# Scores of a wide cross attention on four 32 row strips of the tensor engine, exponentials by pairs of key tiles

## The chip, the cores and the metric

The program runs on one core of a Trainium2 chip, as one launch. Its time is the device time of that core in microseconds; the median of three runs is compared. The engines are named as in the profile: PE is the tensor engine's matmul stream and PEld its weight loads, DVE the vector engine, ACT the scalar engine, POOL GpSimd, SP the engine that issues most transfers. PSUM is the memory that PE writes: eight banks, each of 512 float32 columns.

## What is computed

The reference is a perceiver block: a masked cross attention of 64 latents on 1601 context rows, a gated attention, a quantized feed-forward stage, a second ("wide") cross attention, a laplacian attention, and routed experts. Only the second cross attention is touched:

```python
def _L1_xattn_ref(x, context, context_mask, Wq, Wk, Wv, Wo):
    q = (x @ Wq).reshape(B, N, HEADS, hd).transpose(0, 2, 1, 3)        # 32 batches, N = 64, 16 heads of 16
    k = (context @ Wk).reshape(B, M, HEADS, hd).transpose(0, 2, 1, 3)  # M = 1601, context of width 192
    v = (context @ Wv).reshape(B, M, HEADS, hd).transpose(0, 2, 1, 3)
    scores = jnp.einsum('bhid,bhjd->bhij', q, k) * scale
    scores = jnp.where(context_mask[:, None, None, :], scores, max_neg)
    attn = jax.nn.softmax(scores, axis=-1)
    out = jnp.einsum('bhij,bhjd->bhid', attn, v)
```

## The kernel before

The stages of the block are functions that follow one another with a barrier between them. `wide_cross_attention` is the fourth. It works through 32 batches; the 1601 keys of a batch are 13 tiles of 124 keys (the last has 113), and four chunks of 4, 3, 3 and 3 tiles for the work that goes by chunks. The 256 columns of keys and queries are two halves `o` of 128 rows, 8 heads in each.

For each batch these steps are done, named as in the table `ROUNDS` that sets the order on every engine:

- K(c): PE projects the keys of chunk c into two PSUM banks (five matmuls each), ACT copies them to `khi`, rounded to float32r (a float32 format that PE reads in one pass), DVE writes the rest that was rounded off to `klo`. V0, V1: the values, evicted by ACT into `val`.
- S, X: ACT and DVE split the context of a later batch into the same two parts. Q, Q1, Q2: mask count, `qhi`, `qlo`.
- A(c), c = 0 to 15: scores by `qhi` and `khi` alone, queries as rows, for the maxima. One A is two matmuls (k = 0, 1) of 64 rows each, the upper and the lower half of the array, into two banks; DVE reduces each bank to a column of maxima ("max" below, line 2016).
- mred, M: DVE makes the negated maxima in two bfloat16 parts, PE transposes them (four 128x128 transposes), ACT copies them to `augq`.
- B(t), t = 0 to 12: the exact scores of one key tile, keys as rows, 1024 columns (16 heads of 64 queries) in two banks. Two bfloat16 matmuls of 512 columns lay down mask and maximum (`augk`, `augq`); twelve float32r matmuls of 256 columns add `khi*qhi`, `khi*qlo` and `klo*qhi`. They alternate between the two 64 row halves of the array. ACT takes the exponential into one of four buffers `P`.
- PV(t): 16 heads by `val`, summed in the bank `acc`. F0, F1, F2: the division.

The banks are split so: `sc` is two buffers of two banks, so that B(t+1) is written while ACT reads B(t); `ring` is three banks that K, V, A, M and F1 fill in turn, each fill after the reader of the third fill before it is done (`FILLS`, `room`); `acc` is one. The order is the same on all engines, with B of batch n next to A, K, V of batch n+1 and S, X, Q of batch n+2. The steps that the prediction speaks of stand in these rows of `ROUNDS`:

```python
("Ln", 0), ("Ln", 1), ("A", 0), ("B", 0), ("A", 1), ("B", 1), ("A", 2), ("X", 2), ("K", 1), ("F1", 0), ("PV", 0),
("A", 3), ("B", 2), ("A", 4), ("B", 3), ("S", 3), ("K", 2), ("V0", 0), ("F2", 0), ("Q2", 0), ("PV", 1), ("PV", 2),
("A", 5), ("B", 4), ("A", 6), ("B", 5), ("A", 7), ("X", 3), ("V1", 0), ("V0", 1), ("PV", 3), ("PV", 4),
("A", 8), ("B", 6), ("A", 9), ("B", 7), ("A", 10), ("Sn", 0), ("K", 3), ("V1", 1), ("Qn", 0), ("PV", 5), ("PV", 6),
("A", 11), ("B", 8), ("A", 12), ("B", 9), ("Xn", 0), ("Sn", 1), ("V0", 2), ("V1", 2), ("PV", 7), ("PV", 8),
("A", 13), ("B", 10), ("A", 14), ("B", 11), ("A", 15), ("Sn", 2), ("V0", 3), ("V1", 3), ("mred", 0), ("PV", 9), ("PV", 10),
("B", 12), ("Q1n", 0), ("Xn", 1), ("Kn", 0), ("M", 0), ("PV", 11), ("PV", 12), ("F0", 0)
```

They are called row 1 to row 7 of the schedule below. Each engine takes its own steps from them in this order and waits on semaphores for the others.

## Time and profile before

| | |
|---|---|
| median of three runs | 3859.05 us (3858.34 to 3862.12) |
| the profiled execution | 3861.68 us, of which 3859.9 us between its first and last instruction |
| wide cross attention in it | from about 1900 to 3326 us |
| PE busy over the span | 3103.3 us, 80% |
| DVE, ACT, POOL | 2558.5 us (66%), 1975.3 us (51%), 641.2 us (17%) |

Busy time of PE counts overlapping matmuls once, and the end of a matmul in the trace is modelled. The kernel is a sequence of stages with different limits, so the shares over the whole span say little of one stage; the sections of the trace below are from the wide cross attention, and one from the first cross attention.

### The profile page before, as it was taken

Reading aid. Unit: us, or ns where it says so; the run is one execution under the profiler, and the core shown is the slowest. Engines: PE = TensorE matmul, PEld = TensorE weight load, DVE = VectorE, ACT = ScalarE, POOL = GpSimd, SP = SyncE. Lnnn points to the kernel's source line nnn. Section 1 sums busy time; section 2 is a strip of 40 time slices with the busy share of each in tenths; the row PEclk is TensorE's granted clock in tenths of the full one; section 3 lists DMA queues with packets and bytes.
Section 4 is the critical chain, followed back from the end, with each engine's and each line's share of the span. In section 5 each row is a group of like instructions: output and inputs, shape, how many; then the busy total and the mean of one; then the engine's idle time right before and its main releaser. Section 6 shows DMA issues by size and latency. Waiting matters only on the chain. (4 is left out here: it accounts for less than half of the span.)

```text
span 3859.9 us, 99037 instructions
## 1 busy us (share of the span) xinstructions
PE 3103.3 (80%) x34558; PEld 2704.9 (70%) x34558; DVE 2558.5 (66%) x7485; ACT 1975.3 (51%) x4178; POOL 641.2 (17%) x768
## 2 busy tenths in 40 slices
PE   3449999999999976666399999999999999653574
PEld 3348888888888864444178888888888888542453
DVE  5558888888888845667477777776777777455000
ACT  1146666666766642333146666666666666321111
POOL 0223233233333310000211111111111111000101
PEclk7669999999999986776589999999999999865787
DMA  2132233232233210000111111111111111212511
GB/s 64 51 85 82 81 82 83 80 84 80 79 85 80 78 51 27 14 22 17 38 38 39 41 40 40 40 39 40 38 39 41 39 38 29 73 44 83 180 48 61
DMA packets 235435, 221.25 MB, mean 57 GB/s; under 512 B 69516, under 2 KB 228545, under 8 KB 234816
## 3 DMA queue, kind: packets, MB, share of 16 engines
q1 hardware_dynamic: 232896, 208.22, 19.1%
q0 software_dynamic: 2048, 6.68, 0.5%
q8 instruction: 284, 4.65, 0.5%
q14 instruction: 207, 1.70, 0.1%
HBM read 186.30 MB, written 28.39 MB: 56 GB/s over the span
## 5 line engine op out<-in xcount | busy, mean ns | idle before, releaser
L2016 DVE CUSTOM_DVE_ANT_0 xb_junk<-xb_ring,xb_mbias 128x372 bf16<-128x372 f32 (+2 forms) x1024 | 544.2, 573 | 176.2 <-PE xb_ring L1924 155.3
L1855 ACT ACTIVATE xb_P<-xb_sc 124x1024 f32<-124x1024 f32 (+1 forms) x416 | 426.2, 1027 | 374.5 <-PE xb_sc L1948 372.3
L879 PE MATMUL xa_acc<-xa_raw,xa_P 124*128 124x193 f32 x1664 | 315.6, 330 | 7.2 <-ACT xa_P L754 7.2
L1895 PE MATMUL xb_ring<-xb_xst,xb_whi 128*128 128x372 f32 (+2 forms) x768 | 262.2, 369 | 38.1 <-DVE xb_xst L1995 32.5
L1924 PE MATMUL xb_ring<-xb_khi,xb_qhi 64*128 64x372 f32 (+2 forms) x1024 | 269.0, 404 | 26.6 <-DVE xb_klo L2001 17.3
L1895 PE MATMUL xb_ring<-xb_whi,xb_xst 128*124 128x256 f32 (+1 forms) x1248 | 285.1, 291 | 2.8 <-DVE xb_maxes L2016 0.4
L1948 PE MATMUL xb_sc<-xb_qhi,xb_khi 64*124 64x256 f32 (+1 forms) x1664 | 281.9, 372 | 0.0
L879 PEld LDWEIGHTS xa_acc<-xa_raw,xa_P 124*128 124x128 f32 x1664 | 266.4, 189 | 18.6 <-ACT xa_P L754 12.1
L2001 DVE TENSOR_TENSOR xb_klo<-xb_ring,xb_khi 128x372 fp32r<-128x372 f32 (+2 forms) x256 | 138.6, 571 | 208.8 <-ACT xb_khi L1821 207.8
L865 PE MATMUL xa_sc<-xa_qblk,xa_kT 128*124 128x128 f32 x1664 | 238.6, 272 | 0.0
L1895 PEld LDWEIGHTS xb_ring<-xb_whi,xb_xst 128*124 128x124 f32 (+1 forms) x1248 | 215.8, 187 | 23.1 <-DVE xb_maxes L2016 15.8
L1963 PE MATMUL xb_acc<-xb_P,xb_val 124*17 124x64 f32 x13312 | 229.8, 220 | 0.5 <-ACT xb_P L1855 0.5
L1963 PEld LDWEIGHTS xb_acc<-xb_P,xb_val 124*17 124x17 f32 x13312 | 190.6, 97 | 39.2 <-issue 15.9
L1895 PE MATMUL xb_ring<-xb_wlo,xb_xst 128*124 128x256 f32 (+1 forms) x832 | 217.5, 283 | 0.0
L865 PEld LDWEIGHTS xa_sc<-xa_qblk,xa_kT 128*124 128x124 f32 x1664 | 215.7, 186 | 0.1
L672 POOL CAST xa_kTr<-xa_kT 128x744 fp32r<-128x744 f32 (+1 forms) x128 | 110.1, 860 | 620.1 <-ACT xa_kT L740 620.1
L1948 PE MATMUL xb_sc<-xb_qlo,xb_khi 64*124 64x256 f32 (+1 forms) x1664 | 203.3, 278 | 0.0
L1948 PE MATMUL xb_sc<-xb_qhi,xb_klo 64*124 64x256 f32 (+1 forms) x1664 | 203.1, 277 | 0.0
L1948 PEld LDWEIGHTS xb_sc<-xb_qhi,xb_khi 64*124 64x124 f32 (+1 forms) x1664 | 193.7, 182 | 11.6 <-issue 0.2
L1944 PE MATMUL xb_sc<-xb_augq,xb_augk 64*124 64x512 bf16 (+1 forms) x832 | 199.6, 385 | 0.0
L1924 PEld LDWEIGHTS xb_ring<-xb_khi,xb_qhi 64*128 64x128 f32 x1024 | 151.3, 186 | 65.9 <-DVE xb_klo L2001 29.5
L1895 PEld LDWEIGHTS xb_ring<-xb_xst,xb_whi 128*128 128x128 f32 x768 | 145.6, 192 | 72.2 <-issue 39.3
(435 smaller groups left out, 8342.4 us busy)
## 6 DMA issues: line engine op xcount, KB each, us to landing
xa_raw<-in_ctx SPq DMA_DIRECT2D x64, 279.0 KB
ex_w<-in_W SPq DMA_DIRECT2D x16, 1024.0 KB, 10.0
xa_raw<-in_ctx SPq DMA_DIRECT2D x32, 372.0 KB
xa_xTr<-in_ctxT SPq DMA_DIRECT2D x64, 186.0 KB
xb_raw<-in_ctxT SPq DMA_DIRECT2D x64, 186.0 KB, 2.4
xa_xTr<-in_ctxT SPq DMA_DIRECT2D x32, 248.0 KB, 2.7
xb_raw<-in_ctxT SPq DMA_DIRECT2D x32, 248.0 KB
xa_mask<-in_mask SPq DMA_DIRECT2D x32, 200.1 KB, 5.4
```

Source lines behind the costliest of these rows:

```text
L672: nc.gpsimd.tensor_copy(kTr[:, c % 2, :, 0:W], kT[:, p, :, k0:k0 + W]).then_inc(sem("kTr"), 1)
L865: i = nc.tensor.matmul(s_[0:w, 256 * u + 128 * o:256 * u + 128 * o + 128], kt[:, o, :], qblk[:, t3, o, :], start=False, stop=True, skip_gr ...
L879: i = nc.tensor.matmul(acc[:, o, :], w, raw[0:KEYS, t3, t, :], start=t == 0 and o == 0, stop=t == NKT - 1, skip_group_check=True)
L1855: nc.scalar.activation(P[0:w, pbuf(c, p), :], sc[(c + p) % 2][0:w, :], ACT.Exp).then_inc(sem("exped"), 1)
L1895: i = nc.tensor.matmul(out, l, r, start=k == 0, stop=k == 4)
L1924: i = nc.tensor.matmul(bank[:, 0:w], qhi[half, p, o, 128 * s:128 * s + 128], khi[half, p, o, k0:k0 + w], start=True, stop=True)
L1944: nc.tensor.matmul(s[0:w, 512 * k:512 * k + 512], augk[half, p, keys], augq[half, p, :], start=True, stop=True)
L1948: i = nc.tensor.matmul(s[0:w, 512 * k + 256 * o:512 * k + 256 * o + 256], kk[half, p, o, keys], q[half, p, o, :], start=False, stop=True, ...
L1963: i = nc.tensor.matmul(acc[32 * j:32 * j + VW, 64 * g:64 * g + 64], val[0:w, p, c, h, :], P[0:w, pbuf(c, p), place(h):place(h) + 64], star ...
L2001: v.tensor_tensor(klo[:, p, o, k0:k0 + w], ring[f % 3][:, 0:w], khi[:, p, o, k0:k0 + w].bitcast(F32), ALU.subtract).then_inc(sem("klo"), 1)
L2016: v.tensor_tensor_reduce(out=junk[:, k, 0:w], in0=ring[f % 3][:, 0:w], in1=mbias[:, p, k0:k0 + w], scale=1.0, scalar=-3.0e38, op0=ALU.add, ...
```

## The change

The query rows of B are narrowed from 64 to 32: in each 32 row strip of the array only two heads have their rows, so a matmul needs 128 query columns instead of 256, and four strips (`strip`, `rows`) hold what two halves held. One tile of B is then four bfloat16 matmuls of 256 columns and 24 float32r matmuls of 128 columns, in rounds of four, one in each strip. The four strips write four banks. All four banks of the old two buffers are one buffer `sc` of four banks, and a key tile has half of each bank: the even tile of a pair the columns 0 to 255, the odd tile the columns 256 to 511. PE signals ACT once for a pair of tiles (`NPAIR` = 7 signals a batch), after its second tile; ACT then takes the two exponentials; PE starts the next pair when both are done. A uses the 32 row strips too (still two matmuls of the same columns). M is two transposes instead of four, `augq` has 256 columns instead of 512. The mask row of `augk` is written in four strips by POOL, one after the other, instead of two, and so are its rows of ones at the stage's start.

```diff
-        sc = [m.psum(f"sc{k}", [128, 1024]) for k in range(2)]
+        sc = m.psum("sc", [128, 4, 512])
...
             if not (isinstance(value, int) and value <= 0):
                 engine.wait_ge(sem(name), value)
 
+        def strip(k, s):
+
+            return 2 * k + s
+
+        def rows(r):
+
+            return slice(32 * r, 32 * r + 32)
+
         def place(h):
 
             g, j = h // 4, h % 4
-            return 512 * (g % 2) + 256 * (g // 2) + 64 * j
+            return 256 * strip(g % 2, j // 2) + 128 * (g // 2) + 64 * (j % 2)
 
         block = ctx.enter_context(nc.Block())
 
...
             pool.wait_ge(sem("set"), 1)
-            nc.gpsimd.memset(augk[0:2, :, :], 1.0).then_inc(sem("set"), 1)
-            pool.wait_ge(sem("set"), 2)
-            nc.gpsimd.memset(augk[64:66, :, :], 1.0).then_inc(sem("set"), 1)
-            pool.wait_ge(sem("set"), 3)
-            for k in range(2):
-                nc.gpsimd.memset(negmax[:, :, 64 * k + 32:64 * k + 33], 1.0)
+            for r in range(4):
+                nc.gpsimd.memset(augk[32 * r:32 * r + 3, :, :], 1.0).then_inc(sem("set"), 1)
+                pool.wait_ge(sem("set"), 2 + r)
+            for r in range(4):
+                nc.gpsimd.memset(negmax[:, :, 32 * r:32 * r + 1], 1.0)
             nc.gpsimd.memset(val[:], 1.0).then_inc(sem("set"), 1)
-            pool.wait_ge(sem("set"), 4)
+            pool.wait_ge(sem("set"), 6)
 
             def step(kind, c, n, p):
                 if kind == "Q":
...
-                        pool.wait_ge(sem("s_ps"), (n - 1) * NKT)
+                        pool.wait_ge(sem("s_ps"), (n - 1) * NPAIR)
                     wait_apart(pool)
-                    for k, r in enumerate((32, 96)):
+                    for k in range(4):
+                        r = 32 * k
                         nc.gpsimd.tensor_scalar(augk[r:r + 1, p, :], mask8[r:r + 1, :], -1.0, some[r:r + 1, 1:2], ALU.add, ALU.mult).then_inc(sem("augk"), 1)
-                        pool.wait_ge(sem("augk"), nth(n, 2, k))
+                        pool.wait_ge(sem("augk"), nth(n, 4, k))
                         wait_apart(pool)
             schedule(step, pool)
 
...
-                if kind == "B":
-                    w = KEYS if c < NKT - 1 else LAST
-                    act.wait_ge(sem("s_ps"), nth(n, NKT, c))
-                    upto(act, "pv", nth(n, NKT, c - back(c, p)))
-                    nc.scalar.activation(P[0:w, pbuf(c, p), :], sc[(c + p) % 2][0:w, :], ACT.Exp).then_inc(sem("exped"), 1)
+                if kind == "B" and (c % 2 or c == NKT - 1):
+                    act.wait_ge(sem("s_ps"), nth(n, NPAIR, c // 2))
+                    for t in range(c - c % 2, c + 1):
+                        w = KEYS if t < NKT - 1 else LAST
+                        upto(act, "pv", nth(n, NKT, t - back(t, p)))
+                        half = slice(256 * (t % 2), 256 * (t % 2) + 256)
+                        nc.scalar.activation(P[0:w, pbuf(t, p), :].rearrange("p (r n) -> p r n", r=4), sc[0:w, :, half], ACT.Exp).then_inc(sem("exped"), 1)
                 if kind == "F0":
 
                     act.wait_ge(sem("pv"), nth(n, NKT, NKT - 1))
...
                     pe.wait_ge(sem("qhi"), nth(n, 1, 0))
                     for k in range(2):
-                        half = slice(64 * k, 64 * k + 64)
+                        r = rows(strip(k, s))
                         bank = room((kind, c, k), n)
-                        i = nc.tensor.matmul(bank[:, 0:w], qhi[half, p, o, 128 * s:128 * s + 128], khi[half, p, o, k0:k0 + w], start=True, stop=True)
+                        i = nc.tensor.matmul(bank[:, 0:w], qhi[r, p, o, 128 * s:128 * s + 128], khi[r, p, o, k0:k0 + w], start=True, stop=True)
                         i.then_inc(sem("a_ps"), 1)
                 if kind == "M":
                     pe.wait_ge(sem("negmax"), nth(n, 1, 0))
                     bank = room((kind, c, 0), n)
-                    for a in range(4):
+                    for a in range(2):
                         i = nc.tensor.transpose(bank[:, 128 * a:128 * a + 128], negmax[:, a, :], ident[:])
                     i.then_inc(sem("m_ps"), 1)
                 if kind == "B":
-                    s = sc[(c + p) % 2]
                     w = KEYS if c < NKT - 1 else LAST
                     keys = slice(c * KEYS, c * KEYS + w)
+                    at = 256 * (c % 2)
                     if c == 0:
                         pe.wait_ge(sem("augq"), nth(n, 1, 0))
-                        pe.wait_ge(sem("augk"), nth(n, 2, 1))
+                        pe.wait_ge(sem("augk"), nth(n, 4, 3))
                         pe.wait_ge(sem("qlo"), nth(n, 1, 0))
                         pe.wait_ge(sem("klo"), nth(n, 8, 7))
-                    upto(pe, "exped", nth(n, NKT, c - 2))
-                    halves = [slice(64 * k, 64 * k + 64) for k in range(2)]
-                    for k, half in enumerate(halves):
-                        nc.tensor.matmul(s[0:w, 512 * k:512 * k + 512], augk[half, p, keys], augq[half, p, :], start=True, stop=True)
+                    if c % 2 == 0:
+                        upto(pe, "exped", nth(n, NKT, c - 1))
+                    for r in range(4):
+                        nc.tensor.matmul(sc[0:w, r, at:at + 256], augk[rows(r), p, keys], augq[rows(r), p, :], start=True, stop=True)
                     for kk, q in ((khi, qhi), (khi, qlo), (klo, qhi)):
                         for o in range(2):
-                            for k, half in enumerate(halves):
-                                i = nc.tensor.matmul(s[0:w, 512 * k + 256 * o:512 * k + 256 * o + 256], kk[half, p, o, keys], q[half, p, o, :],
+                            for r in range(4):
+                                i = nc.tensor.matmul(sc[0:w, r, at + 128 * o:at + 128 * o + 128], kk[rows(r), p, o, keys],
+                                                     q[rows(r), p, o, 128 * (r % 2):128 * (r % 2) + 128],
                                                      start=False, stop=True, skip_group_check=True)
-                    i.then_inc(sem("s_ps"), 1)
+                    if c % 2 or c == NKT - 1:
+                        i.then_inc(sem("s_ps"), 1)
                 if kind == "PV":
 
                     w = KEYS if c < NKT - 1 else LAST
```

On PE, two A steps and the B between them at the start of row 4 (A8, B6, A9; the names are output<-inputs, the last pair rows x columns that are written, x the count of equal ones). Before:

```order
L1963 MATMUL xb_acc<-xb_P,xb_val 17x64 x32
L1924 MATMUL xb_ring<-xb_khi,xb_qhi 128x372 x2
L1944 MATMUL xb_sc<-xb_augq,xb_augk 124x512 x2
L1948 MATMUL xb_sc<-xb_qhi,xb_khi 124x256 x4
L1948 MATMUL xb_sc<-xb_qlo,xb_khi 124x256 x4
L1948 MATMUL xb_sc<-xb_qhi,xb_klo 124x256 x4
L1924 MATMUL xb_ring<-xb_khi,xb_qhi 128x372 x2
```

and of the change:

```order
L1977 MATMUL xb_acc<-xb_P,xb_val 17x64 x32
L1936 MATMUL xb_ring<-xb_khi,xb_qhi 128x372 x2
L1956 MATMUL xb_sc<-xb_augq,xb_augk 124x256 x4
L1960 MATMUL xb_sc<-xb_qhi,xb_khi 124x128 x8
L1960 MATMUL xb_sc<-xb_qlo,xb_khi 124x128 x8
L1960 MATMUL xb_sc<-xb_qhi,xb_klo 124x128 x8
L1936 MATMUL xb_ring<-xb_khi,xb_qhi 128x372 x2
```

Nothing stands in another place; B's instructions are twice as many and half as wide. On ACT, rows 4 and 5 of the schedule from the exponentials of B6 and B7 to the value evictions V0(2) and V1(2). The waits are named by the first use of a reused semaphore: here `lp_a_rstd1` is `s_ps`, PE's signal that scores are done, and `lp_qk_ps1` is `pv`, that a buffer `P` is free. Before:

```order
L1855 ACTIVATE xb_P<-xb_sc 124x1024 [waits lp_qk_ps1,lp_a_rstd1] x2
L1812 ACTIVATE xb_xst<-xb_raw 128x496 [waits lp_lT0,lp_x_in1]
L1813 ACTIVATE xb_xst<-xb_raw 64x496
L1821 ACTIVATE xb_khi<-xb_ring 128x362 [waits lp_b_rstd1] x2
L1849 ACTIVATE xb_val<-xb_ring 124x16x16 [waits lp_lT0]
```

and of the change:

```order
L1867 ACTIVATE xb_P<-xb_sc 124x1024 [waits lp_qk_ps1,lp_a_rstd1]
L1867 ACTIVATE xb_P<-xb_sc 124x1024 [waits lp_qk_ps1]
L1822 ACTIVATE xb_xst<-xb_raw 128x496 [waits lp_lT0,lp_x_in1]
L1823 ACTIVATE xb_xst<-xb_raw 64x496
L1831 ACTIVATE xb_khi<-xb_ring 128x362 [waits lp_b_rstd1] x2
L1859 ACTIVATE xb_val<-xb_ring 124x16x16 [waits lp_lT0]
```

Each of the two exponentials waited for its own tile; now the first waits for the whole pair, and the second for no scores at all. What stands behind them on ACT is the same.

## Rows read from the trace of the kernel before

**Rows 1.** The page, busy time by engine.

```profile
PE 3103.3 (80%) x34558; PEld 2704.9 (70%) x34558; DVE 2558.5 (66%) x7485; ACT 1975.3 (51%) x4178; POOL 641.2 (17%) x768
```

**Rows 2.** Windows: stretch, length, busy us (count) by engine, granted clock, DMA share, GB/s.

```profile
2750.00:3050.00 300.00, 295.30 (x5261) 261.60 (x5261) 214.01 (x633) 194.72 (x311) 37.56 (x36) 1.00 0.15 39
```

**Rows 3.** Timeline of PE, M of two batches (start, us from first to last), and M's line.

```profile
2573.33 0.60 PE L1930 MATMUL xb_ring<-xb_ident,xb_negmax 128*128 128x128 f32 x4
...
2616.20 0.60 PE L1930 MATMUL xb_ring<-xb_ident,xb_negmax 128*128 128x128 f32 x4
...
L1930 PE MATMUL xb_ring<-xb_ident,xb_negmax x128: 270/272/328, 1977.5 to 3301.2; 128*128 128x128 f32 x128
```

**Rows 4.** Groups by line and shape, 2000 to 3300 us (busy us, mean ns | idle before).

```profile
L1948 PE MATMUL xb_sc<-xb_qlo,xb_khi 64*124 64x256 f32 x1460 | 182.1, 278 | 0.0
...
L1963 PEld LDWEIGHTS xb_acc<-xb_P,xb_val 124*17 124x17 f32 x11712 | 167.9, 97 | 36.5 <-issue 15.0
...
L1948 PEld LDWEIGHTS xb_sc<-xb_qlo,xb_khi 64*124 64x124 f32 x1460 | 147.4, 182 | 0.0
```

**Rows 5.** Timeline of PE in the last batch, where B follows B.

```profile
3308.79 0.43 PE L1944 MATMUL xb_sc<-xb_augq,xb_augk 64*124 64x512 bf16 x2
...
3309.29 0.40 PE L1948 MATMUL xb_sc<-xb_qlo,xb_khi 64*124 64x256 f32 x4
...
3309.77 0.38 PE L1944 MATMUL xb_sc<-xb_augq,xb_augk 64*124 64x512 bf16 x2
...
3311.81 0.43 PE L1944 MATMUL xb_sc<-xb_augq,xb_augk 64*124 64x512 bf16 x2
```

**Rows 6.** First cross attention, two float32r matmuls of 64 columns, 128 columns of weights each.

```profile
L844 PE MATMUL xa_ring<-xa_klTr,xa_qblkr x64: 191/264/402, 266.3 to 1399.6; 128*128 128x64 f32 x64
...
924.62 0.30 PE L844 MATMUL xa_ring<-xa_klTr,xa_qblkr 128*128 128x64 f32 x2
```

**Rows 7.** Timeline of ACT in rows 4 and 5 of the schedule.

```profile
2597.91 1.03 ACT L1855 ACTIVATE xb_P<-xb_sc 124x1024 f32<-124x1024 f32 x1 [0.18 <-PE xb_sc L1948]
2598.84 0.61 ACT L1812 ACTIVATE xb_xst<-xb_raw 128x496 fp32r<-128x496 f32 x1
...
2599.85 0.81 ACT L1821 ACTIVATE xb_khi<-xb_ring 128x362 fp32r<-128x362 f32 x2
...
2604.15 1.03 ACT L1855 ACTIVATE xb_P<-xb_sc 124x1024 f32<-124x1024 f32 x1 [0.17 <-PE xb_sc L1948]
...
2605.88 0.85 ACT L1849 ACTIVATE xb_val<-xb_ring 124x512 f32<-124x512 f32 x2
```

**Rows 8.** Timeline of DVE there, and from the first max of row 1 of the schedule.

```profile
2595.92 0.55 DVE L2016 CUSTOM_DVE_ANT_0 xb_junk<-xb_ring,xb_mbias 128x372 bf16<-128x372 f32 x1 [1.65 <-PE xb_ring L1924]
...
2597.48 0.54 DVE L2016 CUSTOM_DVE_ANT_0 xb_junk<-xb_ring,xb_mbias 128x372 bf16<-128x372 f32 x1
...
2600.34 0.98 DVE L2001 TENSOR_TENSOR xb_klo<-xb_ring,xb_khi 128x362 fp32r<-128x362 f32 x2 [1.21 <-ACT xb_khi L1821]
...
2618.47 0.67 DVE L2016 CUSTOM_DVE_ANT_0 xb_junk<-xb_ring,xb_mbias 128x496 bf16<-128x496 f32 x1 [0.78 <-PE xb_ring L1924]
...
2623.93 1.00 DVE L2001 TENSOR_TENSOR xb_klo<-xb_ring,xb_khi 128x372 fp32r<-128x372 f32 x2
```

**Rows 9.** Timeline of PE in row 4 of the schedule: A8, A9, K3, A11.

```profile
2595.31 0.43 PE L1924 MATMUL xb_ring<-xb_khi,xb_qhi 64*128 64x372 f32 x2
...
2596.50 0.46 PE L1924 MATMUL xb_ring<-xb_khi,xb_qhi 64*128 64x372 f32 x2
...
2598.08 0.44 PE L1895 MATMUL xb_ring<-xb_xst,xb_whi 128*128 128x362 f32 x1
...
2601.55 0.44 PE L1924 MATMUL xb_ring<-xb_khi,xb_qhi 64*128 64x372 f32 x2
```

**Rows 10.** Timelines of POOL and PE at the start of the stage.

```profile
1910.43 2.76 POOL L1768 MEMSET xb_augk<- 2x3204 bf16 x1
...
1928.13 0.75 PE L1895 MATMUL xb_ring<-xb_xst,xb_whi 128*128 128x496 f32 x1 [32.55 <-DVE xb_xst L1995]
```

More of the change, by code:

```diff
@@ L1803, in _ @@
             nc.scalar.activation(whi[:], w_raw[:], ACT.Copy).then_inc(sem("whi"), 1)
-            act.wait_ge(sem("set"), 4)
+            act.wait_ge(sem("set"), 6)
             def step(kind, c, n, p):
@@ L1836, in step @@
                     if not (isinstance(n, int) and n < 2):
-                        act.wait_ge(sem("s_ps"), (n - 1) * NKT)
-                    nc.scalar.activation(augq[:, p, :], ring[f % 3][:], ACT.Copy).then_inc(sem("augq"), 1)
+                        act.wait_ge(sem("s_ps"), (n - 1) * NPAIR)
+                    nc.scalar.activation(augq[:, p, :], ring[f % 3][:, 0:256], ACT.Copy).then_inc(sem("augq"), 1)
                 if kind in ("V0", "V1"):
@@ L1984, in _ @@
             v.tensor_tensor(wlo[:], w_raw[:], whi[:].bitcast(F32), ALU.subtract).then_inc(sem("wlo"), 1)
-            dve.wait_ge(sem("set"), 4)
+            dve.wait_ge(sem("set"), 6)
             def step(kind, c, n, p):
@@ L2017, in step @@
                                                scale=1.0, scalar=-3.0e38, op0=ALU.add, op1=ALU.max,
[L2018 removed]
+                                               accum_out=maxes[:, p, 4 * o + strip(k, s), c // 4:c // 4 + 1]).then_inc(sem("maxed"), 1)
                 if kind == "mred":
```

20 lines of the change are left out of this document (11 added, 9 removed).

## Prediction

> **What bounds the kernel now.** I read the engines' shares first [rows 1], then the same by stretch: in the wide cross attention PE is busy 295 of 300 us at full clock (1.00 granted), DVE 214, ACT 195 [rows 2]. So there PE sets the time, and a batch is its work: M of one batch starts 42.87 us after M of the one before [rows 3]. The reader is to see one more thing, in the timelines: PE's margin over DVE is thin. In row 4 of the schedule K3 starts at 2598.08, 0.06 us after the max of A9's second bank ended (2597.48 + 0.54), the bank three fills before it in the ring [rows 8, 9]. From A8 to K3 PE already runs in step with DVE.
>
> **B, the tile of scores.** Where B follows B a tile takes 3309.77 - 3308.79 = 0.98 us [rows 5]. Four float32r matmuls, two rounds of two halves, take 0.40 with 0.28 for one [rows 4, 5], so a round is 0.12: 256 columns at 2.4 GHz are 0.107. Six rounds are 0.71; 0.27 is left for the bfloat16 pair of 512 columns and the turn to the next tile. Afterwards a round is four matmuls of 128 columns. If the stream set its length it would be 0.06 and B would fall by 6 x 0.06 and half of 0.213 for the bfloat16 round, 0.46 us in all. But every matmul loads 124 columns of weights first. A load of 17 such columns takes 97 ns, one of 124 takes 182 [rows 4]: 0.79 ns a column, 0.1 us for 124 however many rows it has. One place shows whether it hides: two float32r matmuls of only 64 columns, with 128 columns of weights, take 0.30 together and 0.19 is the shortest single one [rows 6], so the second ends 0.11 after the first, where its stream is 0.03. The load is not hidden. I take 0.105 to 0.11 for a round in all four strips at once: B becomes 0.98 - 0.107 - 6 x 0.01 = 0.81, 0.17 less. The bounds: 0.46 less (stream), 0.11 less (rounds stay at 0.12, only the bfloat16 part gains), and, as no row shows four strips loading at once, rounds of two loads in turn, 0.22, which is 0.5 more.
>
> The Trainium skill says the same of the load: by "TensorE: Matmul & The Clock Gate", section "LDWEIGHTS (loading the stationary operand)", it takes the columns of weights divided by 1.2 per ns, and 32 rows cost what 128 cost. By it the round is 0.103, and B's gain 0.2; the trace agrees, and the rule speaks against a change that halves streams and doubles loads.
>
> **M.** Two transposes of (0.60 - 0.27)/3 = 0.11 fewer [rows 3], 0.22 a batch. If all this reached the end: 13 x 0.17 + 0.22 = 2.4 us a batch, 77 us in 32. It does not, for three reasons.
>
> **DVE is next.** One max is issued every 0.47 us (2595.92 to 2597.48 is three of them with 0.15 idle) [rows 8], an A every 0.94, and A8 to A9 is 1.19, later ones 1.10 [rows 9]. With B shorter PE comes at 0.94 to 1.03 and meets DVE. In rows 3, 4 and 6 of the schedule (three A, two B) the step behind the last A waits for a max whose time is that of the first plus three intervals: only the 0.15 idle goes, not 0.33. Row 1 (496 columns, 0.60 each) is DVE's wholly: its maxes, X2 and klo run without a gap from 2618.47 to 2624.93 [rows 8], so B0 and B1 gain nothing there. What moves it is when A0's first max starts, and M's 0.22 and B12's 0.17 do come before that, as far as klo of Kn0 lets A0 go.
>
> **The pair on ACT.** Before, ACT took the first exponential while PE made the second tile. Row 4: exponential of B7 at 2597.91, two S copies from 2598.84, khi of K3 at 2599.85 to 2600.66, klo of K3 at 2600.34 to 2601.32, and A11 at 2601.55, which may fill the bank that klo frees [rows 7 to 9]: 0.23 us of slack for its second matmul. After, both exponentials start behind B7: 0.93 from one to the next (2597.91 to 2598.84), and B7's end comes 0.2 to 0.3 sooner. ACT's chain is later by 0.93 - 0.3 = 0.6 to 0.7, so A11's second half starts 0.4 to 0.5 later than now. B8 and B9 (0.33 shorter) give most of that back. Then the same in row 5: exponentials of B8 and B9, S, eviction of V0(2) (now 2605.88 to 2606.5) come 0.5 to 0.6 later, while A13, which needs that bank, could go 0.2 sooner: A13's second half is 0.1 to 0.3 late. In rows 2 and 7 the delay is covered by V0 and by PV.
>
> Going through the seven rows, against now: row 1 -0.2 (M's part), row 2 -0.4 at K2, of which Q2 and klo, held up by ACT, leave 0.1 at A5's max; row 3 0; row 4 and 5 together +0.1 to +0.35 at A13; row 6 -0.35 (PE and DVE catch up); row 7 -0.2 (B12) and -0.2 (M, part of it behind klo). A batch becomes 0.3 to 0.8 us shorter, I take 0.53: 30 batches of the steady part, **-16 us**.
>
> **What is added outside.** POOL sets the rows of ones in four pieces of 2.76 us instead of two [rows 10]; DVE and ACT wait for POOL's last signal and PE for them; its first matmul of the stage comes at 1928.13 after 32.55 us of idling: +5.5 us, all exposed, and two more mask rows by POOL beside DVE's first X steps, +0.3. **+6**. In the last batch there is no A to fill PE: a pair of B with its two PV is 3311.81 - 3308.79 = 3.02 us now [rows 5]. Then it is two B, 1.6, the signal 0.2, two exponentials 0.93 + 1.03 [rows 7], and the way back 0.1: 3.7 to 3.8. Six pairs by 0.7: **+4**. The two mask rows that POOL adds in each batch (1.6 us each) start after B12 and end before X2, in PSUM-fed work of DVE: nothing; if DVE's X2 stood in the same time it would pay some tenths of a us a batch.
>
> Sum: -16 + 6 + 4 = -6. The profiled execution took 3861.7 (span 3859.9 and 1.8 around it), so 3855.7 there; the median is 2.6 under that execution: **3853 us**. A difference under 0.2%, 7.7 us, is what a measurement of this kernel can't tell from none, and the forecast is within it.
>
> **Rivals.**
> - Loads hide, so a round costs its stream, 0.06. For it: the halves of B now overlap loads with streams wholly (0.12 a round with loads of 0.1 in it). Against it: rows 6. Then B is 0.52; PE reaches B7, B9 and B3 0.3 to 0.6 sooner, the ACT chains start sooner too, and only DVE's pace and row 1 hold: about 1.9 us a batch, -57, with 10 outside: 3812. Chance 0.07. The Trainium skill has a measured gain for this packing ("TensorE: Matmul & The Clock Gate", "Measured speedup vs the span model": four strips of 32 rows, 512 columns, 3.07 times); by it a round of four here would take 4/3.07 of one stream, 0.07 us, and the sum would be near this rival's, but its streams are four times as long as these.
> - Rounds stay at 0.12, so that B gives 0.11 only, and the pair's delay on ACT shows. Its place is A11 and A13. 0.06 less in each of the seven B's that count and some tenths more wait: 0.4 to 0.6 us a batch, 15 us back: 3868. Slower as soon as a round is 0.12 or an exponential over four half banks takes 0.1 longer than 1.03. Chance 0.18.
> - Four strips do not load together, rounds of 0.2: B 0.3 to 0.5 longer, 4 to 6 us a batch, of which ACT and DVE waits absorb a part: 3980. Chance 0.07.
> - POOL's mask rows or the waits on ACT's queue cost what I set at nothing, beyond row 4 and 5: 0.5 to 1.5 us a batch, 3870 to 3900. Chance 0.1.
>
> **How the numbers follow.** The forecast has 0.58. Its own range is 0.3 to 0.8 us a batch with 10 us outside: 3843 to 3862. In it I give faster (under 3851) 0.45, the same 0.47, slower 0.08. With the rivals: faster 0.26 + 0.07 + 0.02, the same 0.27 + 0.03, slower the rest: 0.35, 0.3, 0.35. Range: it leaves out the serial loads and the hidden loads: 3825 to 3895.
>
> **What would show it.** B beside B at 0.8 (0.5 or 1.0 and more would be a rival); pairs of exponentials 0.93 apart, each pair behind its second tile; PE waiting at A11 and A13 for klo and for V's eviction, at A5, V1 and K3 for maxes; PE's share of the stage falling to some 93%; PE's first matmul of the stage 6 us later; the last batch's pairs 3.75 apart. The prediction is wrong if PE's period falls by over a microsecond, which rows 6 do not allow, or if a wait of ACT's chain repeats in more rows than two.

## The result and the profile after

The changed kernel takes 3870.22 us, median of 13 runs (3863.89 to 3872.02), for 3860.25 us (3856.77 to 3865.34, 13 runs) of the kernel before on the same chip: ratio 1.0023, 95% interval 1.0015 to 1.0032. I had forecast 3853 and no measurable difference. It is slower by 0.15 to 0.32 per cent. The profiled execution took 3867.97 us (span 3866.2), 6.3 more than that of before.

What I read first is whether the mechanism that I had costed is there. The timeline of PE in the last batch, where B follows B, and one row of ACT:

```profile
3306.80 0.33 PE L1956 MATMUL xb_sc<-xb_augq,xb_augk 32*124 32x256 bf16 x4
...
3307.34 0.39 PE L1960 MATMUL xb_sc<-xb_qhi,xb_klo 32*124 32x128 f32 x8
3307.56 0.28 PE L1956 MATMUL xb_sc<-xb_augq,xb_augk 32*124 32x256 bf16 x4
...
3310.48 0.33 PE L1956 MATMUL xb_sc<-xb_augq,xb_augk 32*124 32x256 bf16 x4 [0.27 <-ACT xb_P L1867]
...
3308.49 1.94 ACT L1867 ACTIVATE xb_P<-xb_sc 124x1024 f32<-124x1024 f32 x2 [1.17 <-PE xb_sc L1960]
```

B to B is 3307.56 - 3306.80 = 0.76 us (0.98 in [rows 5]; forecast 0.81). A pair is 3310.48 - 3306.80 = 3.68 (3.02 before; forecast 3.7 to 3.8). The two exponentials of the row, 1.02 us each, start 0.92 apart. All this is near the forecast. Then the steady part, by M's starts, the windows around one of them (columns as in [rows 2]), and the windows of the whole stretch:

```profile
2840.31 0.38 PE L1942 MATMUL xb_ring<-xb_ident,xb_negmax 128*128 128x128 f32 x2
...
2882.29 0.38 PE L1942 MATMUL xb_ring<-xb_ident,xb_negmax 128*128 128x128 f32 x2
...
2925.38 0.38 PE L1942 MATMUL xb_ring<-xb_ident,xb_negmax 128*128 128x128 f32 x2
```

```profile
2880.00:2893.10 13.10, 12.52 (x244) 10.34 (x245) 9.75 (x26) 7.02 (x13) 6.41 (x4) 1.00 0.18 46
...
2893.20:2896.60 3.40, 3.40 (x15) 3.40 (x14) 0.51 (x2) 3.26 (x6) 0.00 (x0) 0.50 0.02 5
...
2896.70:2920.00 23.30, 22.85 (x565) 19.98 (x564) 17.84 (x55) 13.65 (x22) 2.04 (x3) 1.00 0.21 44
...
2750.00:3050.00 300.00, 290.74 (x6526) 252.53 (x6526) 215.72 (x641) 186.99 (x314) 59.14 (x49) 0.99 0.16 40
```

The first batch takes 41.98 us, the second 43.09, and in the second the granted clock is 0.50, that is 1.2 GHz, from 2893.2 to 2896.6, where PE is busy without a break. PE's busy time went from 295.30 to 290.74 of 300 [rows 2], 97% where the forecast had named some 93% as a sign, and the clock's mean went below 1.00, where it had stayed before. The trace's record of the clock has eight such stretches between the first and the last M, outside the turn of the loop; that of before has none.

The turn of the loop (14 batches a pass, two passes) is the other place. PE's first matmul behind it, of before and then of after, and the clock behind it:

```profile
2664.47 0.64 PE L1924 MATMUL xb_ring<-xb_khi,xb_qhi 64*128 64x496 f32 x2 [4.08 <-issue]
```

```profile
2669.36 0.88 PE L1936 MATMUL xb_ring<-xb_khi,xb_qhi 32*128 32x496 f32 x2 [7.25 <-issue]
```

```profile
2664.60:2678.00 13.40, 8.64 (x81) 7.45 (x85) 6.33 (x17) 2.90 (x4) 0.91 (x1) 0.50 0.03 6
2688.50:2691.80 3.30, 3.30 (x18) 3.30 (x17) 2.25 (x7) 2.09 (x3) 0.00 (x0) 0.50 0.41 79
```

PE idles 7.25 us for 4.08, and the half clock in this batch lasts 17.1 us for 3.4. Last, POOL's ones and PE's first matmul of the stage:

```profile
1909.79 11.22 POOL L1777 MEMSET xb_augk<- 3x3204 bf16 x4
...
1935.99 0.75 PE L1907 MATMUL xb_ring<-xb_xst,xb_whi 128*128 128x496 f32 x1 [38.02 <-DVE xb_xst L2009]
```

The four strips of ones take 11.22 us together, and PE idles 38.02 us for 32.55 [rows 10]: 5.5 more, as forecast. The first M comes 81.8 us after the stage's start for 77.7.

From these views a ledger of the stage, changed less before, in the two profiled executions:

- The median of batches in which the clock stayed full is 42.07 us for 42.51: 29 batches by -0.44 = -12.8.
- The batch with the turn takes 53.37 for 48.34: +5.0.
- What the other batches have above their median (after: six with a slow stretch, each 1.0 to 1.5; before: small excesses) is 7.5 for 2.1: +5.4.
- Sum between first and last M: -2.4 (1321.1 for 1323.4). First M +4.1, from the last M to the end +3.6. The stage takes 1431.9 for 1426.5 us.

### The profile page after: what moved, and what is told of

Same layout as the page of the kernel before. It is cut to its first block and busy times, and to the rows that moved or that the text cites. A ratio compares the mean times of both kernels' runs of the same rounds, so it can differ in the third digit from the quotient of the medians.

```text
span 3866.2 us, 110572 instructions
## 1 busy us (share of the span) xinstructions
PE 3073.6 (79%) x40318; PEld 2657.7 (69%) x40318; DVE 2562.6 (66%) x7485; ACT 1933.5 (50%) x4178; POOL 749.8 (19%) x836
## 5 line engine op out<-in xcount | busy, mean ns | idle before, releaser
L1867 ACT ACTIVATE xb_P<-xb_sc 124x1024 f32<-124x1024 f32 (+1 forms) x416 | 405.8, 1024 | 470.6 <-PE xb_sc L1960 470.6
L2031 DVE CUSTOM_DVE_ANT_0 xb_junk<-xb_ring,xb_mbias 128x372 bf16<-128x372 f32 (+2 forms) x1024 | 533.9, 572 | 121.3 <-PE xb_ring L1936 116.0
L1936 PE MATMUL xb_ring<-xb_khi,xb_qhi 32*128 32x372 f32 (+2 forms) x1024 | 350.1, 427 | 48.0 <-DVE xb_klo L2015 22.4
L1804 POOL TENSOR_SCALAR xb_augk<-xb_mask,xb_some 1x1602 bf16<-1x1602 uint8 x128 | 206.7, 1615 | 264.1 <-PE xb_sc L1960 247.5
L1936 PEld LDWEIGHTS xb_ring<-xb_khi,xb_qhi 32*128 32x128 f32 x1024 | 170.0, 184 | 123.7 <-DVE xb_klo L2015 46.3
L1960 PE MATMUL xb_sc<-xb_qhi,xb_khi 32*124 32x128 f32 (+1 forms) x3328 | 241.0, 283 | 0.0
L1960 PE MATMUL xb_sc<-xb_qlo,xb_khi 32*124 32x128 f32 (+1 forms) x3328 | 227.2, 266 | 0.0
L1960 PE MATMUL xb_sc<-xb_qhi,xb_klo 32*124 32x128 f32 (+1 forms) x3328 | 227.2, 266 | 0.0
L1907 PEld LDWEIGHTS xb_ring<-xb_xst,xb_whi 128*128 128x128 f32 x768 | 150.7, 199 | 73.2 <-issue 42.9
L1956 PE MATMUL xb_sc<-xb_augq,xb_augk 32*124 32x256 bf16 (+1 forms) x1664 | 199.6, 297 | 1.6 <-ACT xb_P L1867 1.6
```

The source lines that it names most:

```text
L1804: nc.gpsimd.tensor_scalar(augk[r:r + 1, p, :], mask8[r:r + 1, :], -1.0, some[r:r + 1, 1:2], ALU.add, ALU.mult).then_inc(sem("augk"), 1)
L1867: nc.scalar.activation(P[0:w, pbuf(t, p), :].rearrange("p (r n) -> p r n", r=4), sc[0:w, :, half], ACT.Exp).then_inc(sem("exped"), 1)
L1907: i = nc.tensor.matmul(out, l, r, start=k == 0, stop=k == 4)
L1936: i = nc.tensor.matmul(bank[:, 0:w], qhi[r, p, o, 128 * s:128 * s + 128], khi[r, p, o, k0:k0 + w], start=True, stop=True)
L1956: nc.tensor.matmul(sc[0:w, r, at:at + 256], augk[rows(r), p, keys], augq[rows(r), p, :], start=True, stop=True)
L1960: i = nc.tensor.matmul(sc[0:w, r, at + 128 * o:at + 128 * o + 128], kk[rows(r), p, o, keys], q[rows(r), p, o, 128 * (r % 2):128 * (r % 2) ...
```

## The experiments

All figures of all runs are in one table, since the runs answer each other. "Batch" is the median from M to M of batches at full clock, "slow" the number of stretches at half clock between first and last M outside turns of the loop, "steady" the time from the first M to the last, "stage" the whole fourth stage, all three in the profiled execution. The ratio is to the kernel before on the same chip. The runs come in sets, and the changed kernel was timed in one of them only; where it is compared with a kernel of another set, the difference of the ratios can stand up to 3 us from that of the medians, which the text gives. And a median holds more than the stage: the rest of the kernel, the same code in all sixteen, takes 2428 to 2438 us in the profiled executions (span less stage). Where the expectations count seven slow stretches for the changed kernel they leave out the first batch, and fourteen (e1_ones) and six (e7_both) count one more than the table.

| kernel | median us | ratio (95%) | batch | slow | first M | steady | stage |
|---|---|---|---|---|---|---|---|
| before | 3860.3 | | 42.51 | 0 | 77.7 | 1323.4 | 1426.5 |
| changed | 3870.2 | 1.0023 (1.0015 to 1.0032) | 42.07 | 8 | 81.8 | 1321.1 | 1431.9 |
| changed, ones at once (e1_ones) | 3859.8 | 0.9989 (0.9980 to 0.9998) | 42.01 | 13 | 71.3 | 1324.6 | 1425.0 |
| before, pairs alone (e2_pair_before) | 3907.4 | 1.0119 (1.0103 to 1.0134) | 43.89 | 0 | 76.9 | 1362.1 | 1470.6 |
| changed, no turn (e4_noturn) | 3846.9 | 0.9963 (0.9949 to 0.9977) | 41.87 | 7 | 81.8 | 1304.1 | 1414.9 |
| before, no turn (e5_noturn_before) | 3853.3 | 0.9977 (0.9968 to 0.9986) | 42.54 | 0 | 77.7 | 1317.6 | 1420.7 |
| changed, 64 columns (e3_cols64) | 3879.4 | 1.0042 (1.0027 to 1.0056) | 41.97 | 27 | 81.7 | 1339.0 | 1449.5 |
| changed, 62 keys (e6_keys62) | 3834.3 | 0.9923 (0.9908 to 0.9937) | 41.19 | 3 | 81.8 | 1286.3 | 1394.8 |
| changed, filled (e8_fill) | 3866.0 | 1.0014 (1.0005 to 1.0023) | 42.34 | 0 | 81.7 | 1317.7 | 1429.5 |
| changed, ones, no turn (e7_both) | 3845.8 | 0.9956 (0.9944 to 0.9969) | 41.85 | 5 | 71.3 | 1301.6 | 1402.0 |
| changed, 3 of 4 strips' exp. (e9_exp3) | 3827.6 | 0.9914 (0.9899 to 0.9929) | 40.94 | 4 | 81.3 | 1283.8 | 1391.7 |
| changed, X by two (e10_x2) | 3848.8 | 0.9969 (0.9957 to 0.9981) | 41.52 | 2 | 80.7 | 1297.8 | 1407.5 |
| before, ones, no turn (e11_both_before) | 3848.4 | 0.9968 (0.9956 to 0.9980) | 42.55 | 0 | 71.5 | 1317.6 | 1414.5 |
| changed, ones, no turn, a third filled (e12_best) | 3838.3 | 0.9942 (0.9928 to 0.9955) | 42.06 | 0 | 71.5 | 1302.0 | 1403.2 |
| changed, 4 batches a pass (e13_turn4) | 3905.9 | 1.0112 (1.0095 to 1.0129) | 42.06 | 8 | 81.8 | 1362.9 | 1473.7 |
| before, 4 batches a pass (e14_turn4_before) | 3884.3 | 1.0058 (1.0041 to 1.0074) | 42.52 | 0 | 77.7 | 1348.9 | 1452.0 |

**Changed, ones at once.**

```diff
-            nc.gpsimd.memset(augk[:], 0.0)
+            nc.gpsimd.memset(augk[:], 1.0)
...
-            for r in range(4):
-                nc.gpsimd.memset(augk[32 * r:32 * r + 3, :, :], 1.0).then_inc(sem("set"), 1)
-                pool.wait_ge(sem("set"), 2 + r)
```

> The changed kernel, with the rows of augk for the mask set by one memset of the whole tile to one instead of a memset to zero and four strips of ones (the rows between stand against rows of augq that are zero, so the scores are the same). If the four strips of ones (2.76 us each) stand on the path of the prologue, the first transposes M of the stage come 11 us after the stage's start sooner than in the changed kernel (81.7 us from start to M there, about 71 here) and the whole is 11 us faster, 3859. If the prologue is bound by loads or by X and K anyway, M comes at most 3 us sooner. The steady part must stay as it is (a batch 42.07 us).

The first M comes at 71.3 us, 10.5 sooner, and the median is 10.4 below the changed kernel's. The strips of ones are exposed almost wholly (11.22 us of them). The steady part didn't stay as it was: its batches have 13 slow stretches for 8 and it is 3.5 us longer, with the same instructions in it. So the number of slow stretches moves without any change to what PE does; that has to be kept in mind for every count below.

**Before, pairs alone.**

```diff
-                    act.wait_ge(sem("s_ps"), nth(n, NKT, c))
-                    upto(act, "pv", nth(n, NKT, c - back(c, p)))
-                    nc.scalar.activation(P[0:w, pbuf(c, p), :], sc[(c + p) % 2][0:w, :], ACT.Exp).then_inc(sem("exped"), 1)
+                    if c % 2 or c == NKT - 1:
+                        act.wait_ge(sem("s_ps"), nth(n, NKT, c))
+                        for t in range(c - c % 2, c + 1):
+                            w = KEYS if t < NKT - 1 else LAST
+                            upto(act, "pv", nth(n, NKT, t - back(t, p)))
+                            nc.scalar.activation(P[0:w, pbuf(t, p), :], sc[(t + p) % 2][0:w, :], ACT.Exp).then_inc(sem("exped"), 1)
...
-                    upto(pe, "exped", nth(n, NKT, c - 2))
+                    if c % 2 == 0:
+                        upto(pe, "exped", nth(n, NKT, c - 1))
```

> The kernel before, with one part of the change alone: exponentials by pairs (ACT takes two behind the second tile of a pair, PE waits for both before the next pair); the tiles of scores themselves stay on two halves of 64 rows, 0.98 us. If pairing is cheap in the steady part, because A and X stand between the B's, a batch stays within 0.2 us of 42.49 and only the last batch's pairs grow, from 3.02 to some 4.0 us, +6 us in all, about 3867. If the pair's delay on ACT is what ate the gain of the strips, a batch grows by 0.5 to 1 us, 15 to 30 us more: 3880 and over.

The second holds, and more than it says: pairs alone cost 1.38 us a batch, 45 us in all. The waits from 2000 to 3300 us (total us, times, longest), of before, with pairs alone, and of the changed kernel:

```profile
ACT xb_P L1855 <- PE xb_sc L1948: 357.7, 366, 5.9
...
DVE xb_klo L2001 <- ACT xb_khi L1821: 194.6, 122, 3.0
...
PEld xb_ring L1924 <- DVE xb_klo L2001: 26.3, 58, 0.9
```

```profile
ACT xb_P L1858 <- PE xb_sc L1952: 490.0, 207, 7.8
...
DVE xb_klo L2005 <- ACT xb_khi L1821: 247.3, 119, 3.1
...
PEld xb_ring L1927 <- DVE xb_klo L2005: 47.1, 115, 0.9
```

```profile
ACT xb_P L1867 <- PE xb_sc L1960: 451.1, 213, 11.0
...
DVE xb_klo L2015 <- ACT xb_khi L1831: 245.5, 124, 2.9
...
PEld xb_ring L1936 <- DVE xb_klo L2015: 42.9, 110, 0.7
```

ACT first idles for the pair's second tile, then brings `khi` late, so `klo` is late, and A waits for its bank twice as often (115 times with pairs alone, 110 in the changed kernel, for 58). This is the chain that the prediction described for row 4. Where it costs shows in how long after M the first matmul of each K or V step of the seven rows starts (medians, us):

```
                  row 1   row 2   row 3   row 4   row 5   row 6   row 7   next M
before             4.80   11.14   18.02   24.37   30.34   36.08   40.13   42.51
before, pairs      4.84   11.17   18.41   24.76   31.41   37.48   41.54   43.90
changed            4.59   10.51   17.71   23.89   29.98   35.90   39.70   42.07
3 strips' exp.     4.57   10.49   17.28   23.45   29.19   34.77   38.57   40.94
X by two           4.59    9.97   17.17   23.35   29.44   35.35   39.15   41.52
```

Pairs alone lose 0.36 us in row 3, 0.68 in row 5 and 0.33 in row 6. With pairs in place the strips gain 1.82 us a batch (43.89 to 42.07); the change as a whole is the difference of the two.

**Changed and before, no turn.** `STEADY = 28` for `14` in each.

> The changed kernel with the loop over the steady batches written out whole (STEADY 28 for 14, so there is no turn of the loop). The period that holds the turn is 53.37 us against 42.07 of the others. If the turn's length is what the loop costs (idle issue, then half clock behind it), this kernel is 8 to 11 us faster than the changed one, about 3860. If the slow stretches of the clock come back at another place, as they do at seven places in the steady part already, it gains only the idle 4 to 7 us.

> The kernel before with the loop written out whole. Its turn's period was 48.34 us against 42.49, so it should gain about 6 us: 3854. With the kernel above this tells what of the difference between the two kernels is the turn alone: if the turn is it, changed minus before with no turn is 5 us less than with it (about +5 instead of +10), and if the turn is a matter of chance of the profiled execution, the difference stays at +9.

Without the turn the kernel before is 8.7 us faster and the changed one 23.3, and then the changed one is the faster of the two by 6.4 (3846.9 for 3853.3, same chip). I had expected 8 to 11 for the changed one, and to see it still behind. In the profiled executions it is 21.9: 17.0 in the stage, of which 11.3 in the turn and 0.2 in each other batch (41.87 for 42.07), and 5 outside the stage, where the two kernels are the same. Why a batch is shorter outside a loop no row shows; before, it isn't (42.54 for 42.51).

**Changed, 64 columns, and changed, 62 keys.** The same four of six rounds, cut in the columns streamed or in the columns of weights.

```diff
-                                i = nc.tensor.matmul(sc[0:w, r, at + 128 * o:at + 128 * o + 128], kk[rows(r), p, o, keys],
-                                                     q[rows(r), p, o, 128 * (r % 2):128 * (r % 2) + 128],
+                                hh = kk is khi and q is qhi
+                                wc, wk = (128, w) if hh else (64, w)
+                                i = nc.tensor.matmul(sc[0:wk, r, at + 128 * o:at + 128 * o + wc], kk[rows(r), p, o, c * KEYS:c * KEYS + wk],
+                                                     q[rows(r), p, o, 128 * (r % 2):128 * (r % 2) + wc],
```

That is 64 columns; 62 keys has the same lines but for one:

```diff
+                                wc, wk = (128, w) if hh else (128, w // 2 // 2 * 2)
```

Both leave half of the small products out of the scores.

> The changed kernel, whose four rounds of small products (high keys by low queries, low keys by high queries) stream 64 columns instead of 128; the weights are loaded as before, and half of these small products is left out of the scores. If a round is bound by the loads, B after B in the last batch stays at 0.76 us, though half of the streaming of four rounds in six is gone, and the period of an undisturbed batch stays at 42.1. If the stream bounds the round, B falls to 0.76 - 4 x 0.05 = 0.55. If it is the thin streaming of these rounds that lets the granted clock fall, there are more stretches at half clock in the steady part than the changed kernel's seven (15 or so), and the time is 3875 to 3880 although work was taken out; if the clock has to do with PE's waits, seven again and 3870.

> The counterpart: the same four rounds with 62 columns of weights instead of 124, 128 columns streamed (the other half of the keys has no small products). By the loads a round falls from 0.105 to 0.055, B after B from 0.76 to 0.55; by the stream B stays at 0.76. It also tells what a B shorter by 0.2 is still worth in the steady part: if DVE and ACT's pairs bound it, a batch becomes at most 0.5 us shorter (41.6) of the 13 x 0.2 = 2.6 that PE saves; if PE still bounds it, 39.8.

PE in the last batch, B behind B, with 64 columns and then with 62 keys:

```profile
3330.76 0.33 PE L1956 MATMUL xb_sc<-xb_augq,xb_augk 32*124 32x256 bf16 x4 [0.27 <-ACT xb_P L1867]
...
3331.49 0.31 PE L1956 MATMUL xb_sc<-xb_augq,xb_augk 32*124 32x256 bf16 x4
```

```profile
3280.05 0.33 PE L1956 MATMUL xb_sc<-xb_augq,xb_augk 32*124 32x256 bf16 x4 [0.27 <-ACT xb_P L1867]
...
3280.62 0.29 PE L1956 MATMUL xb_sc<-xb_augq,xb_augk 32*124 32x256 bf16 x4
```

B is 0.73 with half the streaming and 0.57 with half the weights: (0.76 - 0.57) / 4 = 0.048 us a round for 62 columns fewer. The load bounds the round. By the rule of the Trainium skill ("TensorE: Matmul & The Clock Gate", section "LDWEIGHTS (loading the stationary operand)") an estimate for 62 columns is 62 / 1.2 = 0.052 us; the trace agrees with its 0.048. A B shorter by 0.19 is worth 0.88 us a batch of the 2.5 that PE saves: less than PE-bound, more than I expected.

With 64 columns the undisturbed batch is not longer (41.97), but the slow stretches go from 8 to 27 and the time up by 9 us, with work taken out. From 2050 to 2350 us, with 64 columns and in the changed kernel:

```profile
2050.00:2350.00 300.00, 292.99 (x6241) 256.48 (x6239) 205.85 (x606) 181.99 (x304) 59.03 (x49) 0.93 0.15 38
```

```profile
2050.00:2350.00 300.00, 290.46 (x6551) 252.12 (x6552) 215.81 (x639) 188.73 (x316) 59.15 (x49) 0.99 0.16 40
```

PE's busy time in the profile doesn't tell the two apart (and is higher where the clock is lower). What differs is how much is streamed in it.

**Changed, filled.**

```diff
-                                i = nc.tensor.matmul(sc[0:w, r, at + 128 * o:at + 128 * o + 128], kk[rows(r), p, o, keys],
-                                                     q[rows(r), p, o, 128 * (r % 2):128 * (r % 2) + 128],
+                                wide = slice(0, 256) if o == r % 2 else None
+                                i = nc.tensor.matmul(sc[0:w, r, at:at + 256] if wide else sc[0:w, r, at + 128 * o:at + 128 * o + 128], kk[rows(r), p, o, keys],
+                                                     q[rows(r), p, o, wide or slice(128 * (r % 2), 128 * (r % 2) + 128)],
```

> The changed kernel, where every second float32r matmul of B (the one whose 128 columns of output stand beside columns for which its queries are zero) streams 256 columns instead of 128: the same scores, the loads as they are, three halves of the streaming. If a round is 0.105 by its loads, B stays within 0.05 us. If it is the array's idling under these loads that takes the clock down, the stretches at half clock in the steady part (seven in the changed kernel, none before) go away, each gives back 1.0 to 1.5 us, and the time is 3861 to 3865. If the clock falls for the waits of PE, they stay, and the time is 3870 or more.

No slow stretch is left outside the turn. But the added columns aren't free: a batch takes 42.34 for 42.07, 29 x 0.27 = 8 us against 7.5 of the other batches' excess, 0.8 in the last batch before the last M and 2.9 at the turn. The median is 4.2 below the changed kernel's; at 3866.0 it is just above the 3861 to 3865 that I expected, and the intervals of the two ratios overlap.

With the 64 columns this makes the case from both sides: less streamed under the same loads, more stretches; more streamed, none. The counts are of one execution each, and with the streams of the changed kernel they run from 2 to 13 in this table; 27 and 0 lie outside that. The mean granted clock, which every run has, says the same: 0.877 to 0.882 with 64 columns (4 runs), 0.882 to 0.885 in the changed kernel (13), 0.887 to 0.891 filled (11), 0.887 to 0.892 for the kernel before beside it (17).

**Changed and before, ones and no turn; a third filled.** The edits of "ones at once" and "no turn" together in each; in the last kernel every second matmul of `klo` is filled besides.

> The changed kernel with both edits that helped apart: one memset of ones (11 us there) and no turn of the loop (24 us there). If they add up: 3870 - 11 - 24 = 3835. If the first batches only wait for something else, or the stretches at half clock grow in number as they did with the memset alone (fourteen instead of seven), 3840 to 3845.

> The kernel before with the same two edits as the changed kernel in e7_both: one memset of ones and no turn of the loop. Stage by parts: first M 5.5 us earlier than before (72 after the stage's start), the turn 5.8 less: 3861 - 5.5 - 8.5 = 3847. With e7_both at 3845.8 that would make the strips and pairs worth 0 to 2 us where neither the prologue nor the turn counts against them, though a batch there is 41.85 against 42.54 (0.69 x 30 = 21 us): stretches at half clock and the last batch would have to account for the rest. If I have the two causes wrong, it stays at 3853 (as with the turn alone).

> The changed kernel with one memset of ones, no turn of the loop, and 256 columns streamed by every second matmul of the low keys' product alone (a third of the filling of e8_fill). In e8_fill the stretches at half clock were gone but an undisturbed batch took 42.34 instead of 42.07. If the clock needs only a part of the filling, a batch costs 0.1 us more (3 us in all) and the six stretches of e7_both go (7 us): 3840. If a third of the filling leaves the stretches where they are, 3848.

In the medians the two edits don't add: 3845.8 is only 1.1 below "no turn" alone. In the stage they do: it is 12.9 us shorter in the profiled execution (1402.0 for 1414.9), and 8.9 of that are lost outside the stage, in code that is the same. The six runs spread from 3835.5 at a mean granted clock of 0.891 to 3851.4 at 0.884, which would fit a number of slow stretches that varies from run to run; only one run is traced, so this isn't shown. The kernel before with the same edits takes 3848.4, as I had expected.

The kernel with a third of the filling has no slow stretch and takes 3838.3 (3836.4 to 3840.3): 0.6% faster than the kernel before, and 10 us below the kernel before with the same two edits (3846.2 to 3851.4, same chip). What the filling has in this is less sure. Its batch costs 0.21 us (42.06 for 41.85) where I expected 0.1, and in the profiled executions the stage is not shorter with it (1403.2 for 1402.0 without). Its gain stands in the medians alone, 3838.3 for 3845.8; one of the six runs without it was faster than all five with it.

**Changed, exponentials of three strips, and X by two.**

```diff
+            nc.gpsimd.memset(P[:, :, 768:1024], 1.0)
...
-                        nc.scalar.activation(P[0:w, pbuf(t, p), :].rearrange("p (r n) -> p r n", r=4), sc[0:w, :, half], ACT.Exp)
+                        nc.scalar.activation(P[0:w, pbuf(t, p), 0:768].rearrange("p (r n) -> p r n", r=3), sc[0:w, 0:3, half], ACT.Exp)
```

```diff
-                    v.tensor_tensor(xst[0:64, 2, cols], raw[64:128, 0, cols], hi[0][64:128], ALU.subtract)
-                    v.tensor_tensor(xst[64:128, 2, cols], raw[0:64, 1, cols], hi[1][0:64], ALU.subtract).then_inc(sem("xlo"), 1)
+                    i = v.tensor_tensor(xst[0:64, 2, cols], raw[64:128, 0, cols], hi[0][64:128], ALU.subtract)
+                    if first(n):
+                        i = v.tensor_tensor(xst[64:128, 2, cols], raw[0:64, 1, cols], hi[1][0:64], ALU.subtract)
+                    i.then_inc(sem("xlo"), 1)
```

The first leaves out the weights of the fourth strip's four heads, the second one of three subtractions from the second batch on.

> The changed kernel, whose exponentials take three strips of four (768 columns for 1,024, so some 0.2 us less each; P of the fourth strip is set to one once, and the weights of its four heads are left out). Pairing alone cost the kernel before 1.4 us a batch. If what the changed kernel still loses is ACT's chain behind a pair (exponentials, then evictions of K and V for which the banks wait), an undisturbed batch falls from 42.07 by 0.4 to 0.8 us, to 41.3 to 41.7. If DVE's maxes alone hold it, it stays within 0.1 us.

> The changed kernel, whose step X on DVE makes two of its three subtractions (the third part of the low halves of X keeps what the first batch wrote, so part of the correction is left out). DVE has 0.54 to 0.67 us less to do four times a batch, at X0, X1, X2 and X3. If DVE is what the shorter B runs into, an undisturbed batch falls by 0.3 us or more, at X2 in row 1 and X3 in row 3; if it is ACT's chain, by at most 0.1. With less idling of PE the granted clock should fall no more often than in the changed kernel.

An exponential is 0.21 us shorter (groups of ACT by shape, the changed kernel's and this one's):

```profile
L1867 ACT ACTIVATE xb_P<-xb_sc 124x1024 f32<-124x1024 f32 x86 | 83.5, 1024 | 97.5 <-PE xb_sc L1960 97.5
```

```profile
L1868 ACT ACTIVATE xb_P<-xb_sc 124x768 f32<-124x768 f32 x89 | 67.5, 810 | 104.7 <-PE xb_sc L1961 104.7
```

and the batch 1.13 us, more than I had expected, in rows 3, 5, 6 (the table of rows): where pairs alone lose. One subtraction fewer on DVE gives 0.55, all of it in row 2 (behind X2) and none behind it, so nothing at X3 where I had expected some too. So both hold the batch, in different rows, and ACT's pairs the more; neither alone is "the" bound.

**4 batches a pass.** `STEADY = 4`: six turns for one. Open was whether the turn's idle time goes with the loop's length.

> The changed kernel with a loop body of 4 batches (seven passes, six turns) for 14. If a turn is a fixed cost, each takes 11 us as the one did (7.2 of it PE idle at issue): 5 more turns, +55 us, 3925. If the idle goes with the length of the body, it is a third of 7.2 or less at each turn, 2 to 4 us with no or little half clock behind it: +10 to +20 us, 3880 to 3890.

> The kernel before with a loop body of 4 batches. Fixed cost of a turn: 5 more of 5.8 us, 3861 + 29 = 3890, with PE idle 4.1 at each. By the length of the body: 1 to 2 us idle each, 3866 to 3872. Either way the difference of the two kernels per turn (5 us in the profile) is repeated six times here: if it is real and fixed, the changed kernel stands 35 us behind this one; if it goes with the body, some 10 to 15.

One turn of the changed kernel and one of the kernel before, with a body of four batches:

```profile
2957.78 0.88 PE L1936 MATMUL xb_ring<-xb_khi,xb_qhi 32*128 32x496 f32 x2 [7.10 <-issue]
```

```profile
2940.25 0.89 PE L1924 MATMUL xb_ring<-xb_khi,xb_qhi 64*128 64x496 f32 x2 [3.95 <-issue]
```

PE idles about as long as with 14 batches (6.4 to 7.1 us for 7.25, and 3.4 to 4.0 for 4.08 before): it is a fixed cost. A turn's batch is on average 9.0 us above the others in the changed kernel (10.2 or 13.7 us at half clock in each) and 5.5 before (3.4 or 6.8). The median of the kernel before (3884.3) is near what I expected of a fixed cost, 3890. The changed kernel's (3905.9) lies between my two cases: the idle time is fixed, but the one turn that I took the price from (11.3) was dearer than these six are on average. Between the two kernels stand 21.6 us in the medians; I had expected 35 for a fixed cost, and 10 to 15 otherwise.

## Why the prediction was wrong, and where it was right

- **B and the round**: right. 0.76 for 0.81; the load of the weights sets the round, as the two cuts show from both sides. The rivals of hidden loads and of loads in turn are out.
- **Prologue and last batch**: right in mechanism. PE's first matmul 5.5 later, as forecast, the first M 4.1; the last batch 3.6 for 4. The terms written down for a pair (1.6 + 0.2 + 0.93 + 1.03 + 0.1) add up to 3.86 and not to 3.7 to 3.8; measured is 3.68.
- **A batch, row by row**: near in size, 0.44 shorter for 0.53 (0.3 to 0.8), but by some luck. The seven rows as listed add up to 0.7 to 0.95; the 0.53 taken isn't their sum. Up to row 3 they fit: 0.63 gained at K2, 0.31 left behind row 3. A13's second matmul starts 33.46 us after M for 33.35 before (medians), 0.11 late and for the reason forecast; from the 0.31 gained before it that is 0.42 lost, for 0.1 to 0.35. Row 6 gives back 0.29 for 0.35, row 7 gives 0.25 for 0.4. "If a wait of ACT's chain repeats in more rows than two" was written down as what would make it wrong, and it does: rows 3, 5 and 6, where pairs alone lose and shorter exponentials gain.
- **POOL's mask rows**, set at nothing, and the rival that has them cost 0.5 to 1.5 us a batch (3870 to 3900, where the time did fall): a batch of 42.07 leaves no room for that. One thing there did change. In row 5 POOL writes `mbias` (1.61 us) while DVE makes X0, and the first subtraction of X0, 0.67 us where it stands alone, takes longer than before. DVE's X of one batch, before and then after (the longest is that one):

```profile
L1993 DVE TENSOR_TENSOR xb_xst<-xb_raw,xb_xst x5: 529/541/1296, 2830.0 to 2872.7; 64x372 fp32r<-64x372 f32 x3, 64x362 fp32r<-64x362 f32 x1, 64x496 fp32r<-64x496 f32 x1
```

```profile
L2007 DVE TENSOR_TENSOR xb_xst<-xb_raw,xb_xst x4: 529/540/1698, 2828.8 to 2859.0; 64x372 fp32r<-64x372 f32 x2, 64x496 fp32r<-64x496 f32 x1, 64x362 fp32r<-64x362 f32 x1
```

These 0.4 us a batch don't reach the end: with one subtraction fewer in X0 (X by two) row 6 came no sooner than by what row 2 had gained.

- **The step that failed** is the sum "30 batches of the steady part, -16". It took every batch at the full granted clock of [rows 2] and the one turn of the loop as it was. Neither was a term. Measured between first and last M: 12.8 us gained in undisturbed batches, 5.4 given back by batches with stretches at 1.2 GHz, 5.0 by the turn, 2.4 left. Shown by the runs: filling or thinning the streams alone moves the number of stretches from 8 to 0 or 27, and without the turn the changed kernel beats the kernel before. With -2.4 for -16 there, and 7.7 added outside for the 10 forecast, the stage is 5.4 us longer (1431.9 for 1426.5) where 6 less were forecast. The "rounds stay at 0.12" rival gave about the right time (3868) for the wrong reason: B is 0.76 us, and not the 0.87 of that rival.
- **What stood to be seen in advance**: the strips of ones were priced rightly and could have been had for nothing; with one memset of ones the changed kernel is not slower (ratio 0.9989). The kernel before gains from it too, 4.9 us (3853.3 to 3848.4, both without the turn).
- **Open**: the medians differ by 10 us, the profiled executions by 6.3. The granted clock of the changed kernel's other runs (0.882 to 0.885) is no higher than that of the traced one (0.885), which fits more slow stretches in them, but only one execution of each kernel is traced. Why the clock falls in one batch and not in the next, and why their number went from 8 to 13 with one memset, no run shows. Why the turn idles PE 3 us longer with strips isn't settled, only that the length of the body isn't it. Strips without pairs were not run: with this layout PE would write one half of a bank while ACT reads the other.

## What to carry to other kernels

Before a matmul is split into shorter streams on more row strips, count its weight loads: at 124 columns a load of 0.1 us is longer than the 0.05 us of streaming, and then the split buys little time, while PE looks almost as busy as before and streams for less of it. In these runs the granted clock fell with that. Read the granted clock of the changed kernel as a term of its own. Streaming more columns under the same loads took the slow stretches away here, but a batch paid 0.2 to 0.3 us for it, so weigh the two. Read a stage's own time beside the kernel's median when the rest of the kernel varies by 10 us. A PSUM layout that forces the reader to take tiles in pairs costs more than its own delay, since all that stands behind the pair on that engine comes late: here 1.4 us of a batch, for 1.8 that the strips gained.
